# Three one-pass products for four projections, and the next sequence's norm made mid-step

## The reference, cut to what matters

```python
x = x + attn(layernorm(x));  x = x + ffn(layernorm(x))
# attn, per sequence
q = silu(x @ wq);  k = sigmoid(x @ wk);  v = x @ wv        # 256 -> 256 each
decay = 1 - k                                              # with a sign, see theta in the reference
out = scan(S = S * decay + k v;  o = q S)                  # over 512 tokens, 2 heads of 128
out = out * sigmoid(x @ wg1 @ wg2)                         # 256 -> 128 -> 256
out = layernorm(out) * norm_w @ wo                         # 256 -> 256
# ffn: each token goes to the expert with the largest affinity x @ centroids.T
h = relu(layernorm(x) @ w1[e].T + b1[e]);  y = x + h @ w2[e].T + b2[e];  x = alpha * y + (1 - alpha) * x
```

## Time and the profile before

| | before |
|---|---|
| median of 3 runs | 705.01 us (704.4 to 705.52) |
| profiled execution, its own time | 702.75 us |
| its span | 701.0 us |
| attention (to 370 us), sorting (to 401 us), experts (to the end) | 370, 31, 300 us |
| TensorE busy in the whole span | 603.5 us (86%) |
| mean granted clock of TensorE, share of full speed | 0.934 |

### The profile page before, as it was taken

How to read it: one execution, slowest core, us unless ns; L and a number is a source line. 1 busy time by engine, 2 the same in 40 slices (tenths; PEclk the granted TensorE clock), 3 DMA queues, 4 the chain that set the end, 5 groups by cost and what they waited for, 6 DMA issues and landing times.

```text
span 701.0 us, 12512 instructions
## 1 busy us (share of the span) xinstructions
PE 603.5 (86%) x3638; PEld 508.2 (72%) x3639; DVE 347.3 (50%) x864; ACT 278.6 (40%) x671; POOL 221.7 (32%) x384
## 2 busy tenths in 40 slices
PE   4789998989899898997561299999999999999992
PEld 2467775767677576676550199999999999999992
DVE  1476967859586694958427322232333323233231
ACT  3454739465663746654331022222222222222220
POOL 6605160521516034141211203323233332323321
PEclk9999999999999899998865589999999999999997
DMA  8800015032040412021123556546455564645400
GB/s 321 356 32 1 0 31 91 31 58 46 19 90 31 91 31 47 14 70 20 40 53 120 206 215 218 193 173 225 175 204 200 180 228 168 224 178 201 152 28 2
DMA packets 26844, 83.48 MB, mean 119 GB/s; under 512 B 3437, under 2 KB 13039, under 8 KB 20656
## 3 DMA queue, kind: packets, MB, share of 16 engines
q1 hardware_dynamic: 21120, 67.98, 30.2%
q0 software_dynamic: 4992, 14.45, 5.5%
q10 hardware_dynamic: 688, 0.52, 0.2%
HBM read 70.33 MB, written 13.52 MB: 120 GB/s over the span
## 4 chain that ended last, share of the span: by engine, by line
PE 45%; DVE 5%; issue 3%; POOL 1%; DMA 1%; ACT 1%; DVEq 0%; POOLq 0%
PE bank_a L1122 20%; PE bank_c L1136 19%; PE bank_b L1110 1%; DMA arena<-routed_rows,take_now 1%; PE bank_c L992 1%; DVE arena L1420 1%; PE bank_l L878 1%; PE bank_c L985 1%; DVE arena L1197 1%; DVE arena L1186 0%; PE bank_b L970 0%; POOL arena L606 0%; PE bank_a L935 0%; ACT arena L780 0%; ACT arena L783 0%
## 5 line engine op out<-in xcount | busy, mean ns | idle before, releaser
L1447 DVE TENSOR_TENSOR arena<-bank_a,b_col 128x512 f32<-128x512 f32 x78 | 54.0, 692 | 192.3 <-PE bank_a L1122 178.6
L1122 PEld LDWEIGHTS bank_a<-masks,arena 128*128 128x128 f32 x1248 | 147.0, 194 | 1.9
L1122 PE MATMUL bank_a<-masks,arena 128*128 128x128 f32 x1248 | 147.1, 277 | 0.0
L1136 PE MATMUL bank_c<-w_sb,arena 128*128 x624 | 141.4, 380 | 1.4 <-ACT arena L853 0.9
L1136 PEld LDWEIGHTS bank_c<-w_sb,arena 128*128 128x128 f32 x624 | 115.5, 190 | 16.2 <-issue 2.0
L1186 DVE TENSOR_TENSOR arena<-arena 128x256 f32<-128x256 f32 x224 | 92.7, 455 | 36.7 <-PE bank_l L878 36.7
L878 PEld LDWEIGHTS bank_l<-arena,k_mix 128*128 128x128 f32 x448 | 68.9, 205 | 46.1 <-issue 22.5
L890 PE MATMUL bank_a<-arena 128*128 128x512 f32 x160 | 86.3, 639 | 14.2 <-ACT arena L679 14.2
L853 ACT ACTIVATE arena<-arena 128x512 f32<-128x512 f32 x78 | 45.0, 622 | 107.1 <-PE bank_c L1136 102.7
L878 PE MATMUL bank_l<-arena,k_mix 128*128 128x128 f32 x448 | 75.4, 295 | 12.2 <-ACT k_mix L679 7.0
L843 ACT ACTIVATE masks<-bank_b,b_col,g_col 128x128 f32<-128x128 f32 x78 | 31.5, 453 | 132.6 <-PE bank_b L1110 132.6
(11 more groups left out here) (137 smaller groups left out, 751.1 us busy)
## 6 DMA issues: line engine op xcount, KB each, us to landing
arena<-w SPq DMA_DIRECT2D x39, 1024.0 KB, 4.8
routed_rows<-arena SPq DMA_DIRECT2D x8, 1026.0 KB, 8.5
arena<-x SPq DMA_DIRECT2D x16, 512.0 KB, 4.2
w_sb<-w SPq DMA_DIRECT2D x8, 1024.0 KB, 14.7
arena<-b SPq DMA_DIRECT2D x1, 1024.0 KB, 4.7
arena<-routed_rows,take_now POOLq DMA_INDIRECT x39, 4.2
out<-k_mix,put_now POOLq DMA_INDIRECT x39, 2.5
arena<-wk SPq DMA_DIRECT2D x1, 256.0 KB, 3.8
```

The lines of the kernel that those rows point to most:

```text
L1122: m = pe.matmul(bank_a[k // 4][:, k % 4 * P:(k % 4 + 1) * P], w1_now[t.par][:, i * F + k * P:i * F + (k + 1) * P], xl_t[t.par % 2][:, i * ...
L1136: m = pe.matmul(bank_c[p][:, 0:D], h_act[:, k * P:(k + 1) * P], w2_sb[:, bass.ds(e * (FC * D) + k * D, D)], start=(k == 0), stop=(k == FC ...
L1447: dve.tensor_tensor(h_sb[:, n * 512:(n + 1) * 512].rearrange("p (k t) -> p k t", t=P), bank_a[n][:, :].rearrange("p (k t) -> p k t", t=P), ...
```

## The change

The k, q, v, gate and output projections no longer use float32 matmuls. Each operand is split into a high part, rounded to the type F32R (a float32 that TensorE takes in rounded form), and a low part, the rounded rest. A product is the sum of three matmuls on such parts: high x high, low x high, high x low. The two gate weights are multiplied into one 256 x 256 matrix at the start, v and the gate become one product with 512 output columns (`v_gate`), and `g1_proj`, `g1_copy`, `v_proj` and `gate_proj` go. The high part of the normed input is ScalarE's copy out of PSUM that was there before; the low part is a new VectorE instruction (`xn_low_part`), and the same holds for the attention output (`o_low_part`). The parts of the weights are made in step 0.

In the orders of the engines: VectorE's `x_stats(nxt)` moves from behind the last level to behind level 2; GpSimd's norm of the next input moves from the end of the step to its start, and the q and k product goes ahead of `double_norm`; ScalarE's `x_norm(nxt)` moves from the end of the step to behind level 6. In step 8 the output norm of the last sequence is made at the step's end and not in step 9. Half of `w2` now lies where the attention's buffers were, and is fetched when the last projection is done (step 8).

The core of the diff (names of semaphores, buffers and the code of step 0 are cut where they repeat a pattern):

```diff
@@ tensor: the products
-            def channels(w, width, h, bank, i):
-                return pe.matmul(bank[:, :], w[:, i * width + h * P:i * width + (h + 1) * P], xn_t[:, i * T:(i + 1) * T],
-                                 start=(i == 0), stop=(i == DC - 1))
+            def channels(high, low, h, bank, i):
+                x = slice(i * T, (i + 1) * T)
+                w = slice(i * D + h * P, i * D + (h + 1) * P)
+                pe.matmul(bank[:, :], high[:, w], xn_high[:, x], start=(i == 0), stop=False)
+                pe.matmul(bank[:, :], low[:, w], xn_high[:, x], start=False, stop=False)
+                return pe.matmul(bank[:, :], high[:, w], xn_low[:, x], start=False, stop=(i == DC - 1))
             def k_proj(a, h, i):
                 need(pe, s_xnt, DC, a, max(h, i) + 1)
+                need(pe, s_xlo, DC, a, max(h, i) + 1)
+            def v_gate(a, j):
+                if j < 2:
+                    need(pe, s_q, H, a, j + 1)
+                else:
+                    need(pe, s_v, TJ, a, j - 1)
+                    need(pe, s_gate, TJ, a, j - 1)
+                for i in range(DC):
+                    x = slice(i * T + j * P, i * T + (j + 1) * P)
+                    w = slice(i * 2 * D, (i + 1) * 2 * D)
+                    pe.matmul(bank_a[j % 2][:, :], xn_high[:, x], wvg_high[:, w], start=(i == 0), stop=False)
+                    pe.matmul(bank_a[j % 2][:, :], xn_high[:, x], wvg_low[:, w], start=False, stop=False)
+                    m = pe.matmul(bank_a[j % 2][:, :], xn_low[:, x], wvg_high[:, w], start=False, stop=(i == DC - 1))
+                m.then_inc(s_vg, 1)
             def out_proj(c, half, j):
                 need(pe, s_ont, DC, c, DC)
+                need(pe, s_olo, DC, c, DC)
...
@@ tensor: order behind level 6
                 of(a, q_proj, 1, 1)
-                of(a, g1_proj, 0)
+                if b is None and a is not None:
+                    gate_weights()
+                    pe.wait_ge(s_whigh, 4)
+                    pe.wait_ge(s_wlow, 4)
+                of(a, v_gate, 0)
                 of(b, k_transposes)
-                of(a, g1_proj, 1)
+                of(a, v_gate, 1)
                 of(b, key_values)
-                of(a, v_proj, 0)
-                of(a, v_proj, 1)
-                of(a, gate_proj, 0)
+                of(a, v_gate, 2)
...
                 of(c, x1_transposes)
-                of(a, gate_proj, 1)
+                of(a, v_gate, 3)
                 of(a, diagonal, 0)
@@ vector
+            def xn_low_part(a, i):
+                need(dve, s_xnt, DC, a, i + 1)
+                x = slice(i * T, (i + 1) * T)
+                dve.tensor_tensor(xn_low[:, x], bank_a[i][:, :], xn_high[:, x], ALU.subtract).then_inc(s_xlo, 1)
...
                     of(b, update, l, 0)
+                    if l == 0:
+                        of(a, xn_low_part, 0)
                     if l > 0:
                         of(b, pick, l - 1)
                     of(b, update, l, 1)
+                    if l == 0:
+                        of(a, xn_low_part, 1)
...
                 level(2)
+                of(nxt, x_stats)
                 level(3)
                 of(a, decays, 0)
                 level(4)
+                of(c, o_low_part, 0)
+                of(c, o_low_part, 1)
                 of(a, q_mult, 0)
...
-                of(nxt, x_stats)
                 of(b, states)
@@ scalar
                 for l in (5, 6):
                     for h in range(H):
                         of(b, mix, l, h)
+                of(nxt, x_norm)
                 of(a, q_sigmoid, 1)
                 of(b, k_tok_copies)
...
-                of(a, gate_sigmoid, 1)
-                of(nxt, x_norm)
+                of(a, v_copy, TJ - 1)
+                of(a, gate_sigmoid, TJ - 1)
                 of(a, mix, 0, 0)
                 of(a, mix, 0, 1)
+                if a is None and b is not None:
+                    for j in range(TJ):
+                        o_norm(b, j)
                 of(c, rows_of)
@@ sync
+                if a is None and b is not None:
+                    need(sp, s_dz, H, b, H)
+                    fetch_w2(range(E // 2))
```

More of the change, by code:

```diff
@@ L582, in step @@
             def step(a, b, c, nxt):
-                if c is not None:
+                if c is not None and b is not None:
                     need(pool, s_on, TJ, c, 0)
                     norm("o", c)
+                if nxt is not None:
+                    need(pool, s_xn, TJ, nxt, 0)
+                    norm("x", nxt)
                 if a is not None:
@@ L830, in _ @@
             x_norm(Step(0, 0, 2))
+            act.wait_ge(s_wk, 16)
+            copy(wk_high, wk_sb).then_inc(s_whigh, 1)
+            act.wait_ge(s_wq, 16)
+            copy(wq_high, wq_sb).then_inc(s_whigh, 1)
+            act.wait_ge(s_wo, DC)
+            copy(wo_high, wo_sb).then_inc(s_wohigh, 1)
             pipeline(act, step)
@@ L900, in q_proj @@
                 need(pe, s_k, H, a, h + 1)
[L901 removed]
+                m = channels(wq_high, wq_low, h, bank_a[h], i)
                 if i == DC - 1:
                     m.then_inc(s_qz, 1)
[L905 to L921 removed]
@@ L923, in gate_proj, with gate_weights @@
-            def gate_proj(a, half):
-                need(pe, s_g1, 1, a, 1)
-                need(pe, s_v, 2, a, half + 1)
-                for j in range(2):
-                    t0 = (2 * half + j) * P
-                    m = pe.matmul(bank_a[1 - half][:, j * D:(j + 1) * D], g1_t[:, t0:t0 + P], wg2_sb[:, :], start=True, stop=True)
-                m.then_inc(s_gz, 1)
+            def gate_weights():
+                pe.wait_ge(s_wvg, 48)
+                for i in range(DC):
+                    m = pe.transpose(bank_b[1][:, i * P:(i + 1) * P], wg1_sb[:, i * P:(i + 1) * P], ident[:, :])
+                m.then_inc(s_w1t, 1)
+                pe.wait_ge(s_w1tc, 1)
+                for i in range(DC):
+                    m = pe.matmul(bank_b[0][:, i * D:(i + 1) * D], wg1_t[:, i * P:(i + 1) * P], wg2_sb, start=True, stop=True)
+                m.then_inc(s_w12, 1)
@@ L947, in key_values @@
             def key_values(b):
[L948 removed]
+                need(pe, s_v, TJ, b, TJ)
                 for c in range(TJ - 1):
```

218 lines of the change are left out of this document (128 added, 90 removed).

## The result

The changed kernel takes 714.51 us (median of 4 runs, 713.41 to 720.39) for 704.70 of the kernel before: ratio 1.015, interval 1.01 to 1.02. The profiled execution of the changed kernel is the longest of the four (span 718.6 us; the other spans are 711.7 to 713.5), so the trace shows 17.6 us more than the one of before and the medians 9.8.

The account below looks back on a forecast made before the run. VectorE was taken to fill the levels and TensorE the time behind the last `q_mult`. From a profiled 702.75 us, -3.7 for the steps and +6.3 for the clock gave 705.4, 707.7 as median; band 702 to 713, range 693 to 721.

Parts of the forecast that it names:

- Full step without a fall of the clock: Each full step of the changed kernel was to take 39.9 us, the one without `x_stats` 38.3.
- Behind the last `q_mult`: Rest of a full step after VectorE's last `q_mult`, filled by `v_gate` pieces: 13.1 us instead of 14.04.
- The VectorE stretch: From VectorE's first `update` to its last `q_mult` in a full step: 25.9 us instead of 22.14, bounds 25 and 27.2.
- The old waits to be recovered: VectorE's existing waits in the levels, 1.3 us per full step, were to vanish into the added work.
- the forecast of -5.5 us: Sum over the six full steps without clock falls: 237.8 us against 243.3.
- The clock: Falls after TensorE's new waits before `out_proj(0, 0)` and `v_gate` 1 were to cost +6.3 us, bounds none and +19.5.
- step 0: Program start: weight splits and gate weights (ending about 26 us) put the first `update` at 38.2 us, +1.8 us.
- Steps 8 and 9: Last steps: +1.5 us for `o_low_part` and its wait, then -0.4 us from rounded matmuls replacing 16 records.
- Rival 1: Same full steps but no clock drops: 701.3 us, down to 693 if the new waits vanish too; chance 0.27.
- rival 3: Clock drops at both new waiting places in nearly every full step: 721 us; chance 0.15.
- Rival 2: Levels are bound by TensorE, so its relief counts: 659 us, or 680 if half passes through; chance 0.13.
- Rival 4: A rounded matmul takes 0.43 us on TensorE, some 6 us more per full step: 740 us; chance 0.03.

Follow-up runs that it names:

- e2_out_fp32: The changed kernel with the output projection back in one fp32 matmul per channel block, without o_low and its wait: 686.50 us.
- e7_spare_subtractions: e2_out_fp32 plus two unused 128x512 VectorE subtractions per step where o_low was made, without TensorE's wait for them: 695.82 us.
- e5_norm_at_tail: e2_out_fp32 with the next sequence's statistics, norm and `x_norm` put back behind the last `q_mult`: 677.68 us.
- e3_two_products: The changed kernel without the third product (high weights by low part of x) in k and q: 721.98 us.
- e4_out_later: The changed kernel with each `out_proj` block one place later in TensorE's order, behind `level(5, 0)` and following: 703.0 us, ratio 0.998.
- e10_q_first: e5_norm_at_tail with VectorE's `q_mult(1)` ahead of last pick and residuals, `x_stats` ahead of x1's statistics, GpSimd's next norm ahead of `double_norm`: 667.14 us.
- e12_early_vg_x1_on_act: e9_q_first_early_vg with x1's two copies back on ScalarE: 668.24 us.
- e8_early_vg: e5_norm_at_tail with the first v|gate tile moved between the levels and x1's two copies moved from ScalarE to VectorE: 682.80 us.
- e9_q_first_early_vg: e10_q_first with the first v|gate tile early and x1's copies on VectorE, as in e8_early_vg: 685.87 us.

## Why the prediction was right, and where its sizes were off

**The sign and its reason held, the size less.** Forecast 707.7 us, measured 714.5, 1.5 us above the band (702 to 713) of the forecast itself. The prediction had VectorE as the bound in the levels, TensorE's relief worth nothing there, and the price of the removed stall paid back by VectorE's new work, a new wait and the clock. In experiments, each adding one part, for a full step at full clock:

| part | full step | median |
|---|---|---|
| fp32, norm in the tail, new GpSimd order | 36.31 | 675.45 |
| + rounded k, q, v\|gate | 36.54 | 677.68 |
| + statistics, norm and `x_norm` mid-step | 37.75 | 686.50 |
| + two subtractions as for `o_low` | 38.96 | 695.82 |
| + TensorE's wait for them (the changed kernel) | 40.7 | 714.51 |

Against the first row the change pays 39 us; the removed stall gives 29; the difference is the loss of 10. Half of the payment, 18.7 us, is the last row, the wait with the falls of the clock (and the rounded `out_proj` itself, which is less work, and the split of wo in step 0).

**Terms, forecast against the trace.** Full step without a fall of the clock: 39.9, measured 40.7. Behind the last `q_mult`: 13.1, measured 13.1. The VectorE stretch: 25.9, measured 27.85 in step 2 (76.47 to 104.32) and 26.83 in step 3; **this term was mis-sized**, in its part "0.7 us" for `level(5, 0)` behind `out_proj(0, 0)`: it is 0.98 us at full clock and 2.06 at half. The old waits to be recovered were 1.01 us and not 1.3 (the trace of step 2 has 0.43 and two of 0.29, where the prediction counts three), and one of 0.29 stayed, so that term was too kind by 0.6 us. Over six steps the forecast of -5.5 us became -0.4: five of 40.7 and step 7 at 39.4 are 242.9 us for 243.3. The 39.4 is an estimate, 40.7 less the 1.3 us by which step 7 is the shorter in e2_out_fp32 and in e7_spare_subtractions. The clock: forecast 6.3 us, measured 7.1 (250.0 us for the six, less 242.9). I had put three falls before `out_proj(0, 0)` and one before `v_gate` 1; there were four and one.

**The largest miss is step 0.** Forecast +1.8 - 1.1 = +0.7 us up to the first `update` of step 2, measured 76.47 for 70.38, +6.1; nearly all of it, +5.96, is there at the first `update` of step 1 (42.36 us for 36.40, where I had 38.2). I placed the gate weights' end at 26 us; it was 29.3, since I let `x_norm(nxt)` move at no cost and didn't see that in step 0 its new place is ahead of those weights on ScalarE. In e5_norm_at_tail, where it stands behind them, the step is 3.64 us shorter than in e2_out_fp32, and the clock does not fall in it (the statistics and the norm are moved there too, so the share of each isn't shown). Steps 8 and 9 cost 3.4 us for 1.1, and all of the excess is in step 8, +3.8 us for +1.5: there the wait before `out_proj` was 2.80 us, and what followed ran at the low clock. The sorting and the experts, which the change does not touch, took 1.3 us more; no run isolates that. 6.1 + 6.7 + 3.4 + 1.3 is the trace's 17.6 us within rounding; as the profiled execution had a lower clock than the others (0.926 for 0.934 to 0.938), part of it isn't in the median.

**What was luck in it.** The forecast's loss came from the clock alone: without it the sum was -3.7 us. In the trace the five falls in the full steps make 7.1 of the 17.6 us, and the parts outside the full steps, which I had at +0.7 and +1.1, make 9.5. So the sign would have held with no fall in the full steps (9.8 us less 7.1), against what I had written, and what carries it is in good part a term that I had near nothing.

**Rivals.** Rival 1 (no falls) and rival 3 (falls everywhere) missed the count of falls: it was five, in four of the six steps. Rival 2 (TensorE's relief counts) is false for this order: one product less gives 40.58 us for 40.64. For another order it is true in part: with VectorE's new order the rounded kernel's step is 34.78 us for 36.31, so 1.5 of the 3.3 us that TensorE is spared count. That is 9 us over six steps, of which 3.1 are given back before step 2 (70.67 for 67.58). So part of the relief was there to be had; what hid it was an order in which TensorE waits for the last row of VectorE's stretch. Rival 4 (0.43 us a matmul): measured 0.23.

The Trainium skill ("TensorE: Matmul & The Clock Gate", section on the back-to-back issue gap) gives a sustained 131 ns for a 512-wide matmul. The rows above say 0.23 us (104.71 to 104.94, at clock 1.00), so it does not hold for rounded fp32 parts, and the forecast's 0.216 was 6% short. Of the lock in "SBUF — State Buffer" (section "SBUF: two separate sides") this trace again shows nothing: the root of the next norm ran on GpSimd from 88.20 to 89.24, and the `update` pair at 88.62 took 0.75 us, as elsewhere.

**Left open.** Why the clock falls behind one wait of 2.65 us and not behind the next of the same length. How much of the 18.7 us between the last two rows of the table is the clock and how much the wait: in the profiled execution the six full steps are 17.6 us longer than in e7_spare_subtractions, 10.4 by the wait (1.74 a step) and 7.1 by the five falls; the other executions, with their higher clock, were not traced. A kernel with rounded `out_proj` but without the wait was not run.

## What to carry to other kernels

Ask of every edit which engine is full at its place: work added there counts nearly whole (1.21 us for two subtractions of 1.28 us, and 1.2 for the 1.6 us of `x_stats` in the rounded kernel, but 0.7 to 1.1 for the same in the fp32 one), work taken from the other engine counts only once the order no longer makes it wait for the full engine's last row. A wait put ahead of a matmul that the full engine itself depends on is paid twice, and once more if the clock falls. And when a stall is the reason for a change, first remove the stall alone: here a new order of GpSimd's instructions was worth 29 us, more than the change it was packed with could pay for; with the rounded products and `q_mult` first it became 667.1 us, the fastest kernel of this study.

## What the runs showed of the hardware that I had not expected

- Less work did not make the program faster, and by the medians it was slower: 1.84 us less of matmuls per step, 7.5 us more, with ranges that meet. In its trace TensorE's clock fell to 0.50 at two places in each of three steps (137 and 150 us in one of them in e3_two_products), in the changed kernel's in one. All four of its executions had a lower mean clock (0.908 to 0.923) than any of the changed kernel (0.926 to 0.938).
- The clock also fell behind a wait of 1.18 us (170.75 us in e4_out_later), after waits of 0.91 and 0.78 us in the 5 us ahead of it. It never fell in the full steps of e2_out_fp32, e5_norm_at_tail, e7_spare_subtractions, e10_q_first and e12_early_vg_x1_on_act, where TensorE's longest wait was 1.5 us. But the length of the longest wait doesn't decide: it stayed up behind the waits of 2.07 to 2.09 us of e8_early_vg, and it fell in three full steps of e9_q_first_early_vg (at 138.7, 213.8 and 254.8 us), 1.5 to 3.2 us behind waits of 0.51 and 0.65 us, the longest there.
- A matmul on rounded fp32 parts takes 0.23 us for 512 columns at full clock (0.12 for 256), 0.43 at half, and the fp32 product 0.86: three rounded pieces (0.69) cost 0.8 of one fp32 product.
- At the start of the program a row of the clock can say 1.00 while the matmuls run at the half pace. In the changed kernel, TensorE's timeline and a window:

```profile
16.17 0.63 PE L944 MATMUL bank_a<-xn_low,wk_high 128*128 128x512 f32 x1
16.60 0.63 PE L942 MATMUL bank_a<-xn_high,wk_high 128*128 128x512 f32 x1
21.55 0.40 PE L942 MATMUL bank_a<-xn_high,wq_high 128*128 128x512 f32 x1
21.78 0.40 PE L943 MATMUL bank_a<-xn_high,wq_low 128*128 128x512 f32 x1
```

```profile
16.00:18.00 2.00, 2.00 (x6) 1.52 (x6) 1.50 (x8) 0.43 (x1) 2.00 (x8) 1.00 1.00 418
```

They start every 0.43 us up to 21 us and every 0.23 behind it. The trace's first record of the clock begins at 21.3 us, where the pace changes; before it the 1.00 stands for no record. So the pace of equal rows tells the clock there, and the granted clock doesn't.
